# Two silu activations of a Mamba and mixture-of-experts kernel put into one block on ScalarE

## The chip, the cores and the metric

The kernel runs on one core of a Trainium2 chip. The metric is the device time of one execution in microseconds (us), lower being better. The program uses five engines of the core that run side by side and meet only at semaphores: TensorE (PE in the profile, with its weight loads as PEld), VectorE (DVE), ScalarE (ACT), GpSimd (POOL) and SyncE (SP), which here only starts transfers.

## The reference

The input is 32 sequences of 512 tokens with 256 features. A Mamba layer comes first and a mixture of 64 experts with a shared expert second, each after a layer norm and each added to its input. Cut to what the change is about:

```python
xz = xn @ in_proj_w.T
xp, z = xz[..., :D_INNER], xz[..., D_INNER:]
xc = silu(causal_conv(xp) + conv_b)
y = selective_scan(xc, softplus(dt), -exp(A_log), Bm, Cm, D)   # h = exp(dt*A)*h + dt*u*B ; y = <h, C>
m = gelu((y * silu(z)) @ out_proj_w.T)                          # silu of z
...
gu = x @ shared_gate_up_w
shared = silu(gu[:, :Is]) * gu[:, Is:] @ shared_down_w          # silu of the shared expert's gate
```

The scan has 512 channels (4 blocks of 128 partitions) and 16 states for each channel, so each sequence needs 64 scans of 128 x 512, done two at a time.

## The kernel before

The main part is a software pipeline over the 32 sequences. One turn handles the scan of sequence b, the preparation of sequence b+1 (`prep_at`: norm, projections of x and z, convolution, step sizes) and what comes after the scan of sequence b-1 (`post_at`: output projection, gelu, gated unit, second norm, router, shared expert). A turn has 32 half-steps (NS = 32, numbered s = 0 to 31), one for each pair of channel blocks and each of the 16 states. Each engine has a function `turn` of its own that walks through the 32 half-steps; the constants at the end of the file (`Z_AT`, `SILU_Z`, `SU_AT` and so on) say by hand in which half-step an engine issues which extra piece of work. An engine executes strictly in that order, and there is no planner. Turns 0, 1, 30 and 31 are written out, turns 2 to 29 are a hardware loop with two turns in its body, so there is a jump after every second turn. Turn 0 has no `post_at`, turn 31 no `prep_at`, so 30 turns have both.

In half-step s

- ScalarE first computes the decays of half-step s+2 (`decays`, L515, two activations into one of two PSUM buffers `state[n % 2]`). It must wait until VectorE has finished half-step s in that buffer (for the half-steps in `ON_POOL` the scan itself, otherwise the read-out).
- VectorE runs the scan (L1400), and in half-steps not in `ON_POOL` also the read-out with C (L1410). Among 25 to 31, the half-steps 25, 27, 28 and 29 are in `ON_POOL`.
- GpSimd makes the scan's inputs three half-steps ahead (L392) and does the read-outs of the half-steps in `ON_POOL` one half-step behind (L401).
- TensorE adds up the read-outs two half-steps behind (`add_up`, L907), then does the extra matmuls of `post_at`, then those of `prep_at`.

Around the change the hand-written order is this. The shared expert's gate is projected in half-steps 19, 20, 21 and 23 (`SG_AT`, L1015) and copied from PSUM by ScalarE one half-step later (`read_gate`, L673). `hid_silu` (L677) follows in half-step 24. The up-projections come in 25 to 28 (`SU_AT`, also L1015), and VectorE multiplies each one into `hid` one half-step later (`mul_up`, L1357), the first after waiting for `hid_ready`. The down-projection (`shared_down`, L1023) comes in 29 and 30 and is read by VectorE in 30 and 31 (`add_shared`, L1363). z is projected in 14, 21, 22 and 25 (`Z_AT`, L938), copied one half-step later (`read_z`, L579), and `silu_z` (L597) follows in 27. VectorE uses silu of z only in the next turn (`gate_y`, L1313). `choose` (L1341 to L1351, the router's top 8) stands on VectorE in half-step 25, `scales_x` (L520 to L527) on ScalarE in 26, `weights` (L660, L663) on ScalarE in 29.

Silu, and the exponential of the decays, need different activation tables. A switch is an instruction of its own, ACT_TABLE_LOAD: the load of the silu table stands at the line of the silu (L677, L597), the load back at L497, in `use_exp_ln`.

Of the kernel before, what the change touches and what calls it, by code (L numbers as in the profile page):

```python
# [40 lines left out]
def mamba_moe(nc, x, vectors, in_wT, conv_w, x_wT, dt_wT, a_log, out_wT, glu_wT, router_w, sgu_w, sdown_w, expert_w, out, counts, table, bc):  # L41
    ctx = ExitStack()
    with ctx:
# [451 lines left out]
        def _(act):  # L495
            def use_exp_ln():
                act.preload_act_table_set("natural_log_exp_and_others")  # L497
# [39 lines left out]
            def norm_x(p):  # L537
                act.wait_ge(scales0_ready, 5 * p + 5)
                wait(act, prep_full, (p - 1) * PREP_USES - FIRST + PREP_T[1] + 1)
                wait(act, post_read, (p - 1) * POST_USES - POST_USES)  # L540
                for i in range(NT):
                    m = act.activation(xn[:, i, :], xin[:, i, :], ACT.Identity, bias=shift[:, 1, i:i + 1],
                                       scale=rstd[:, 1, i:i + 1])
                m.then_inc(ln0, 1)

            def sum_x(p, h):
                wait(act, post_read, (p - 2) * POST_USES + POST_MT[1] + 1)
                for i in range(NT):
                    m = act.activation(xs[h][:, i, :], xin[:, i, :], ACT.Identity, bias=shift[:, 0, i:i + 1],
                                       scale=keep[:, i:i + 1])  # L550
                m.then_inc(xs_ready, 1)
# [9 lines left out]
            def read_xnT(p, f):  # L561
                act.wait_ge(prep_full, p * PREP_USES - FIRST + PREP_T[f] + 1)
                act.activation(xnT[:, f, :], prbank, ACT.Identity, bias=b_sb[:, f:f + 1],
                               scale=g_sb[:, f:f + 1]).then_inc(prep_read, 1)

            def begin_conv(p, h, j):
                act.wait_ge(prep_full, p * PREP_USES - FIRST + PREP_X[j] + 1)
                if j % JH == 0:
                    hf = j // JH
                    wait(act, summed, (p - 1 - hf) * NS + hf * N + 1)  # L570
                    wait(act, dt_ready, 4 * (p - 1 - hf) + 2 * hf + 1)
                act.activation(conv_part(h, j), prbank, ACT.Identity, bias=cb_sb[:, j:j + 1],
                               scale=cw_sb[:, j, PAD:TAPS]).then_inc(conv_begun, 1)

            def read_z(p, h, j):
                act.wait_ge(prep_full, p * PREP_USES - FIRST + PREP_Z[j] + 1)
                if j == 0:
                    wait(act, post_full, (p - 2) * POST_USES + POST_Y[J - 1] + 1)
                act.copy(sz[h][:, j, :], prbank).then_inc(prep_read, 1)  # L579

            def silu_x(p, h):
                act.wait_ge(prep_read, p * PREP_USES - FIRST + PREP_X[J - 1] + 1)
                both = xc3[:, h:h + 2, :, :]
                act.activation(both, both, ACT.Silu).then_inc(xc_ready, 1)
# [8 lines left out]
            def silu_z(p, h):  # L593
                if isinstance(p, int) and p == 0:
                    act.wait_ge(first_sz, J)
                wait(act, prep_read, p * PREP_USES - FIRST + max(PREP_Z) + 1)
                act.activation(sz[h][:, :, :], sz[h][:, :, :], ACT.Silu).then_inc(z_ready, 1)  # L597

            def read_xd(p):
                act.wait_ge(prep_full, p * PREP_USES - FIRST + PREP_S + 1)  # L600
                wait(act, bc_stored, 16 * p)
                act.copy(xd[0:64, :], prbank[0:64, :]).then_inc(prep_read, 1)

            def read_dt(p, j):
                act.wait_ge(prep_full, p * PREP_USES - FIRST + PREP_D[j] + 1)
                if j % JH == 0:
                    wait(act, input_ready, (p - 1) * NS + (j // JH + 1) * N)
                act.activation(dtu[:, j, :], prbank, ACT.Abs, bias=db_sb[:, j:j + 1])
                act.activation(dt[:, j, :], prbank, ACT.Relu, bias=db_sb[:, j:j + 1]).then_inc(prep_read, 1)  # L609
# [8 lines left out]
            def soft_log(p, hf):  # L618
                part = dtu[:, JH * hf:JH * hf + JH, :]
                act.wait_ge(soft, 4 * p + 2 * hf + 1)  # L620
                act.activation(part, part, ACT.Ln, bias=1.0).then_inc(soft, 1)
# [68 lines left out]
            def prep_at(p, h, s):  # L690
                if s == NORM0:
                    norm_x(p)
                if s == SUM_X:
                    sum_x(p, h)
                for f in range(FM):
                    if s == T_AT[f] + AFTER_T:
                        read_xnT(p, f)
                for j in range(J):
                    if s == X_AT[j] + AFTER_X:
                        begin_conv(p, h, j)  # L700
                    if s == Z_AT[j] + AFTER_Z:
                        read_z(p, h, j)
                if s == SILU_X:
                    silu_x(p, h)
                    use_exp_ln()
                if s == SILU_Z:
                    silu_z(p, h)
                    use_exp_ln()
                if s == S_AT + AFTER_S:
                    read_xd(p)  # L710
                for j in (0, 1):
                    if s == D_AT[j] + AFTER_D:
                        read_dt(p, j)
                if s == SOFT_AT[0][0]:
                    soft_exp(p, 0)
                if s == SOFT_AT[0][1]:
                    soft_log(p, 0)
                if s == SKIP_AT[0]:
                    scale_skip(p, h, 0)

            def post_at(q, h, s):
                for j in range(J):
                    if s == Y_AT[j] + AFTER_Y:
                        read_y(q, j)
                for f in range(FM):
                    if s == M_AT[f] + AFTER_M:
                        read_m(q, f)
                if s == M_AT[1] + AFTER_M:
                    gelu(q)
                    use_exp_ln()  # L730
                for f in range(FM):
                    if s == G_AT[f] + AFTER_G:
                        read_g(q, f)
                if s == G_AT[1] + AFTER_G:
                    glu_gate(q)
                    use_exp_ln()
                if s == SCALES2:
                    scales_x1(q)
                if s == NORM2:
                    norm_x1(q)  # L740
                for f in range(FM):
                    if s == XT_AT[f] + AFTER_XT:
                        read_x2T(q, f)
                for k in range(KS):
                    if s == SG_AT[k] + AFTER_SG:
                        read_gate(q, k)
                if s == SILU_HID:
                    hid_silu(q)
                    use_exp_ln()
                if s == ROUTER_EXP:  # L750
                    router_exp(q)
                if s == WEIGHTS:
                    weights(q)
                if s == C_AT + AFTER_C:
                    read_counts(q)

            def turn(b, h, prep, post):
                for s in range(NS):
                    to = ahead(b, h, s, 2, prep)
                    if to:  # L760
                        decays(*to)
                    second_steps(b, h, s)
                    if isinstance(b, int) and b == 0 and s == FIRST_SILU_Z:
                        silu_z(0, 0)
                        use_exp_ln()
                    if post:
                        post_at(b - 1, 1 - h, s)
                    if prep:
                        prep_at(b + 1, 1 - h, s)
                    if s == SCALES0 and not (isinstance(b, int) and b + 2 >= B):  # L770
                        scales_x(b + 2)

# [116 lines left out]
        def _(pe):  # L889
# [137 lines left out]
            def prep_at(p, h, s):  # L1027
# [3 lines left out]
                for j in range(J):  # L1031
                    if s == X_AT[j]:
                        project_in(p, PREP_X[j], j)
                    if s == Z_AT[j]:
                        project_z(p, j)
# [569 lines left out]
NORM2 = 16  # L1605
T_AT = (1, 3)
X_AT = (4, 5, 10, 12)
Z_AT = (14, 21, 22, 25)
SKIP_AT = (31, 14)
SILU_X = 14  # L1610
SILU_Z = 27
SILU_HID = 24
S_AT = 16
D_AT = (17, 18, 0, 1)
SOFT_AT = ((19, 21), (1, 3))
# [21 lines left out]
D_LATE = tuple(at + (NS if i >= JH else 0) for i, at in enumerate(D_AT))  # L1637
PREP_T, PREP_X, PREP_Z, (PREP_S,), PREP_D, PREP_USES = order(T_AT, X_AT, Z_AT, (S_AT,), D_LATE)
FIRST = PREP_USES - JH
# [39 lines left out]
```

## Time and profile before

| what | value |
|---|---|
| runs | 4388.48, 4369.52 and 4387.80 us; median 4387.8 us |
| profiled execution | 4384.62 us |
| its span, first to last instruction | 4381.6 us |
| mean granted TensorE clock | 0.893 of full speed |
| busy: GpSimd / VectorE / TensorE / ScalarE | 90% / 86% / 82% / 73% of the span |
| table loads at L497 / L597 / L677 | 159 / 32 / 31 |

Everything below is read from the profiled execution. Its time lies 3.0 us above its span, and 3.2 us below the median of the runs. In the timelines a line gives the start and the duration in us, then engine, line of the kernel, operation, output and input tiles, shapes and a count; a bracket at the end gives the idle time of the engine just before the instruction and the instruction that ended it. Several equal instructions in a row are merged.

### The profile page before, as it was taken

How to read it: one execution, taken by the hardware profiler on the slowest of the kernel's cores; microseconds unless marked ns; L12 is line 12 of the kernel's file. 1: busy time of each engine (PE TensorE's matmuls, PEld its weight loads, DVE VectorE, ACT ScalarE, POOL GpSimd, SP SyncE). 2: the span in 40 equal slices, each digit the busy share in tenths (PEclk: the TensorE clock that was granted, in tenths of full speed). 3: DMA queues.
4: the chain of work that ended last, by engine and by line, in shares of the span. 5: the costliest groups of instructions: out<-in, count | busy, mean ns of one | idle time of the engine just before them, and what ended most of it. 6: DMA issues, size and time to landing. Idle time of an engine off the chain costs nothing.

```text
span 4381.6 us, 54679 instructions
## 1 busy us (share of the span) xinstructions
PE 3579.6 (82%) x16225; PEld 2342.4 (53%) x16225; DVE 3752.6 (86%) x3728; ACT 3217.0 (73%) x5179; POOL 3951.1 (90%) x1931
## 2 busy tenths in 40 slices
PE   5788888888888888888888888888888888887765
PEld 3455555555555555555555555555555555554554
DVE  6899899898989989898998989898898989999432
ACT  6678777777777777777787777777777777776343
POOL 6999999999999999999999999999999999999266
PEclk8899989899989989998998989899898989998887
DMA  3232212133221222232222223222222322321576
GB/s 128 92 104 99 94 64 100 60 103 104 102 101 63 95 83 77 104 104 99 89 68 94 74 96 104 101 103 79 79 89 71 103 104 99 104 62 43 132 181 134
DMA packets 133417, 414.49 MB, mean 95 GB/s; under 512 B 21577, under 2 KB 80073, under 8 KB 100185
## 3 DMA queue, kind: packets, MB, share of 16 engines
q1 hardware_dynamic: 111720, 358.50, 22.4%
q0 software_dynamic: 21360, 51.92, 6.5%
q8 instruction: 161, 2.64, 0.2%
q14 instruction: 176, 1.43, 0.1%
HBM read 326.88 MB, written 50.46 MB: 86 GB/s over the span
## 4 chain that ended last, share of the span: by engine, by line
POOL 54%; issue 28%; PE 7%; DVE 5%; ACT 3%; DMA 3%; POOLq 1%; DVEq 0%; SPq 0%; ACTq 0%
POOL hs L392 33%; POOL hs L401 15%; POOL dtu L416 3%; DVE ps L1400 2%; DMA out<-hs,dt 2%; DVE hs L1400 1%; PE ps L907 1%; PE ps L1023 1%; POOL dt L411 1%; POOL out L474 1%; ACT ps L515 1%; PE ps L896 1%; PE ps L951 1%; DMA hs<-table,dt 1%; ACT L497 0%
## 5 line engine op out<-in xcount | busy, mean ns | idle before, releaser
L392 POOL TENSOR_TENSOR hs<-dtu,b_all 128x1024 f32<-128x1024 f32 x1024 | 2425.3, 2404 | 47.2 <-PE ps L907 44.7
L515 ACT ACTIVATE ps<-dt,neg_a 128x512 f32<-128x512 f32 x2048 | 1326.0, 683 | 437.9 <-DVE hs L1400 227.8
L1400 DVE TENSOR_TENSOR_SCAN hs<-ps,hs 128x1024 f32<-128x1024 f32 x512 | 1167.5, 2281 | 195.5 <-ACT ps L515 138.1
L907 PEld LDWEIGHTS ps<-ident,hs 128*128 128x128 f32 x8192 | 1038.7, 152 | 513.3 <-issue 401.3
L401 POOL TENSOR_TENSOR hs<-hs,c_all 128x1024 f32<-128x1024 f32 x512 | 1216.2, 2376 | 78.9 <-DVE hs L1400 78.9
L907 PE MATMUL ps<-ident,hs 128*128 128x128 f32 x8192 | 1168.1, 293 | 102.4 <-issue 58.0
L1400 DVE TENSOR_TENSOR_SCAN ps<-ps,hs 128x1024 f32<-128x1024 f32 x512 | 1170.0, 2285 | 74.0 <-ACT ps L515 69.9
L1410 DVE TENSOR_TENSOR hs<-ps,c_all 128x1024 f32<-128x1024 f32 x512 | 626.2, 1223 | 34.0 <-DVE ps L1400 6.6
L1015 PE MATMUL ps<-mT,w_sgu 128*128 128x512 f32 x992 | 482.9, 609 | 90.7 <-ACT hid L673 48.2
L931 PE MATMUL ps<-xnT,w_in 128*128 128x512 f32 x496 | 251.3, 631 | 81.6 <-DVE xc L1304 80.8
L1304 DVE SCALAR_TENSOR_TENSOR xc<-ps,cw_sb,xc 128x509 f32<-128x509 f32 (+2 forms) x384 | 285.3, 743 | 24.1 <-ACT xc L793 11.3
L1015 PEld LDWEIGHTS ps<-mT,w_sgu 128*128 128x128 f32 x992 | 168.7, 190 | 235.4 <-issue 119.1
L977 PE MATMUL ps<-mT,w_glu 128*128 128x512 f32 x496 | 242.5, 611 | 51.9 <-ACT mT L635 42.3
L938 PE MATMUL ps<-w_in,xnT 128*128 128x512 f32 x496 | 278.8, 691 | 3.7 <-ACT sz L579 3.7
L1023 PE MATMUL ps<-w_sd,hid 128*128 128x256 f32 x992 | 228.9, 384 | 16.3 <-DVE mT L1363 16.2
L968 PE MATMUL ps<-hid,w_out 128*128 128x512 f32 x496 | 223.3, 593 | 0.2 <-ACT hid L625 0.2
L1023 PEld LDWEIGHTS ps<-w_sd,hid 128*128 128x128 f32 x992 | 183.4, 190 | 48.4 <-DVE mT L1363 23.7
L497 ACT ACT_TABLE_LOAD x159 | 204.0, 1283 | 3.6 <-PEq L1649 0.8
L985 PE MATMUL ps<-ident,hid 128*128 128x128 f32 x248 | 59.2, 385 | 179.5 <-DVE xn L1325 178.1
L931 PEld LDWEIGHTS ps<-xnT,w_in 128*128 128x128 f32 x496 | 89.7, 191 | 203.7 <-DVE xc L1304 120.8
L951 PE MATMUL ps<-xd,w_dt 32*128 32x512 f32 x252 | 169.4, 757 | 23.7 <-ACT dt L609 21.8
L962 PE MATMUL ps<-ident,sz 128*128 128x128 f32 x496 | 96.4, 328 | 85.6 <-DVE sz L1313 63.9
(196 smaller groups left out, 4448.8 us busy)
## 6 DMA issues: line engine op xcount, KB each, us to landing
b_all<-bc SPq DMA_DIRECT2D x128, 1024.0 KB, 6.1
c_all<-bc SPq DMA_DIRECT2D x128, 1024.0 KB, 7.7
dt<-dtu POOLq DMA_DIRECT2D x63, 512.0 KB, 4.7
c_all<-expert_w SPq DMA_DIRECT2D x64, 384.0 KB, 3.9
table<-rows SPq DMA_DIRECT2D x32, 640.0 KB, 3.8
xin<-x SPq DMA_DIRECT2D x32, 512.0 KB, 3.6
out<-mT SPq DMA_DIRECT2D x32, 512.0 KB, 3.9
bc<-xd SPq DMA_DIRECT2D x32, 64.0 KB, 1.6
```

Source lines behind the costliest of these rows:

```text
L392: pool.tensor_tensor(ring(h, hf, n), dtu[:, JH * hf:JH * hf + JH, :], b_all[:, n, :].unsqueeze(1).broadcast_to([P, JH, L]), ALU.mult)\
L401: pool.tensor_tensor(ring(h, hf, n), ring(h, hf, n), c_all[:, n, :].unsqueeze(1).broadcast_to([P, JH, L]), ALU.mult)\
L515: i = act.activation(state_of(n)[:, k, :], dt[:, j, :], ACT.Exp, scale=neg_a[:, j, n:n + 1])
L907: m = pe.matmul(ybank[:, i, k * P:(k + 1) * P], ring(h, hf, n)[:, k, i * P:(i + 1) * P], ident[:, :], start=False, stop=(n == N - 1), is_t ...
L931: m = pe.matmul(prbank, w_in[:, f, col * P:(col + 1) * P], xnT[:, f, :], start=(f == 0), stop=(f == FM - 1))
L938: m = pe.matmul(prbank, xnT[:, f, i * P:(i + 1) * P], w_in[:, f, DI:2 * DI], start=(f == 0), stop=(f == FM - 1))
L977: m = pe.matmul(pobank, w_glu[:, k, col:col + P], mT[:, k, :], start=(k == 0), stop=(k == FM - 1))
L1015: m = pe.matmul(pobank, w_sgu[:, f, block * P:(block + 1) * P], x2T[:, f, :], start=(f == 0), stop=(f == FM - 1))
L1023: m = pe.matmul(po_tok[:, i, :], hid[:, k, (2 * c + i) * P:(2 * c + i + 1) * P], w_sd[:, k, :], start=(k == 0), stop=(k == KS - 1))
L1304: dve.scalar_tensor_tensor(conv_part(h, j)[:, back:L], bank[:, 0:L - back], cw_sb[:, j, k:k + 1], conv_part(h, j)[:, back:L], ALU.mult, AL ...
L1400: dve.tensor_tensor_scan(inputs if s in ON_POOL else whole, whole, inputs, 0.0, ALU.mult, ALU.add).then_inc(state_ready, 1)
L1410: dve.tensor_tensor(ring(h, hf, n), state_of(n), c_all[:, n, :].unsqueeze(1).broadcast_to([P, JH, L]), ALU.mult)\
```

## The change

`hid_silu` and `silu_z` move from half-steps 24 and 27 into half-step 25, one behind the other, with one load of the exponential table behind both in place of one behind each. So that z is complete by then, its last projection moves from half-step 25 to 24, and the copy that follows it from 26 to 25. In half-step 25 ScalarE then issues in this order: decays of half-step 27, `hid_silu` (from `post_at`), the copy of the last part of z and `silu_z` (from `prep_at`), `use_exp_ln`.

```diff
                 if s == SILU_X:
                     silu_x(p, h)
                     use_exp_ln()
-                if s == SILU_Z:
+                if s == SILU_BOTH:
                     silu_z(p, h)
-                    use_exp_ln()
...
-                if s == SILU_HID:
+                if s == SILU_BOTH:
                     hid_silu(q)
-                    use_exp_ln()
...
                     if prep:
                         prep_at(b + 1, 1 - h, s)
+                    if s == SILU_BOTH:
+                        use_exp_ln()
...
-Z_AT = (14, 21, 22, 25)
+Z_AT = (14, 21, 22, 24)
...
-SILU_Z = 27
-SILU_HID = 24
+SILU_BOTH = 25
```

## Rows read from the trace of the kernel before

**Rows 1.** The page: busy times, and the chain that ended last, by line.

```profile
PE 3579.6 (82%) x16225; PEld 2342.4 (53%) x16225; DVE 3752.6 (86%) x3728; ACT 3217.0 (73%) x5179; POOL 3951.1 (90%) x1931
...
POOL hs L392 33%; POOL hs L401 15%; POOL dtu L416 3%; DVE ps L1400 2%; DMA out<-hs,dt 2%; DVE hs L1400 1%; PE ps L907 1%; PE ps L1023 1%; POOL dt L411 1%; POOL out L474 1%; ACT ps L515 1%; PE ps L896 1%; PE ps L951 1%; DMA hs<-table,dt 1%; ACT L497 0%
```

**Rows 2.** Table of waits, whole run: waiter, releaser, total us, times, longest.

```profile
DVE ps L1400 <- ACT ps L515: 69.9, 88, 3.0
```

**Rows 3.** Timeline of ScalarE in half-steps 24 to 29 of one turn.

```profile
2028.08 1.30 ACT L515 ACTIVATE ps<-dt,neg_a 128x512 f32<-128x512 f32 x2 [0.36 <-DVE hs L1410]
...
2029.92 1.28 ACT L677 ACT_TABLE_LOAD   x1
2031.21 1.91 ACT L677 ACTIVATE hid<-hid 128x2048 f32<-128x2048 f32 x1
...
2036.96 0.57 ACT L579 COPY sz<-ps 128x512 f32<-128x512 f32 x1
...
2038.51 1.30 ACT L515 ACTIVATE ps<-dt,neg_a 128x512 f32<-128x512 f32 x2 [0.31 <-DVE hs L1400]
...
2041.12 1.92 ACT L597 ACTIVATE sz<-sz 128x2048 f32<-128x2048 f32 x1
2043.06 1.28 ACT L497 ACT_TABLE_LOAD   x1
2044.36 2.53 ACT L515 ACTIVATE ps<-dt,neg_a 128x512 f32<-128x512 f32 x4
```

**Rows 4.** Timeline of VectorE in half-steps 25 to 31 of the same turn.

```profile
2027.96 2.28 DVE L1400 TENSOR_TENSOR_SCAN hs<-ps,hs 128x1024 f32<-128x1024 f32 x1
...
2035.60 0.68 DVE L1357 TENSOR_TENSOR hid<-ps,hid 128x512 f32<-128x512 f32 x1
2036.19 2.28 DVE L1400 TENSOR_TENSOR_SCAN hs<-ps,hs 128x1024 f32<-128x1024 f32 x1
...
2038.97 2.28 DVE L1400 TENSOR_TENSOR_SCAN hs<-ps,hs 128x1024 f32<-128x1024 f32 x1
...
2043.95 0.67 DVE L1357 TENSOR_TENSOR hid<-ps,hid 128x512 f32<-128x512 f32 x1
2045.69 2.30 DVE L1400 TENSOR_TENSOR_SCAN ps<-ps,hs 128x1024 f32<-128x1024 f32 x1 [1.07 <-ACT ps L515]
...
2049.16 0.87 DVE L1363 SCALAR_TENSOR_TENSOR mT<-ps,small,xn 128x256 f32<-128x256 f32 x2
...
2053.84 0.88 DVE L1363 SCALAR_TENSOR_TENSOR mT<-ps,small,xn 128x256 f32<-128x256 f32 x2 [0.35 <-PE ps L1023]
```

**Rows 5.** Timeline of TensorE in the same turn.

```profile
2028.98 1.91 PE L907 MATMUL ps<-ident,hs 128*128 128x128 f32 x16
2030.73 1.88 PE L1015 MATMUL ps<-mT,w_sgu 128*128 128x512 f32 x4
2032.45 1.88 PE L938 MATMUL ps<-w_in,xnT 128*128 128x512 f32 x4
...
2050.09 3.72 PE L1023 MATMUL ps<-w_sd,hid 128*128 128x256 f32 x16 [0.39 <-DVE mT L1363]
```

**Rows 6.** Timeline of VectorE in turn 31, which has no `prep_at`.

```profile
4049.19 0.67 DVE L1357 TENSOR_TENSOR hid<-ps,hid 128x512 f32<-128x512 f32 x1
...
4053.83 0.88 DVE L1363 SCALAR_TENSOR_TENSOR mT<-ps,small,xn 128x256 f32<-128x256 f32 x2 [0.51 <-PE ps L1023]
```

**Rows 7.** Timeline of GpSimd behind a jump, and behind a turn's end without one.

```profile
2061.24 2.34 POOL L401 TENSOR_TENSOR hs<-hs,c_all 128x1024 f32<-128x1024 f32 x1 [0.98 <-DVE hs L1400]
...
2073.97 2.36 POOL L392 TENSOR_TENSOR hs<-dtu,b_all 128x1024 f32<-128x1024 f32 x1 [3.43 <-PE ps L907]
...
2216.42 2.35 POOL L401 TENSOR_TENSOR hs<-hs,c_all 128x1024 f32<-128x1024 f32 x1 [0.77 <-DVE hs L1400]
```

**Rows 8.** Line L497 (ns min/median/max, first to last start); ScalarE, 4150 to 4380 us, by line.

```profile
L497 ACT ACT_TABLE_LOAD  x159: 1283/1283/1283, 0.8 to 4076.9; - x159
...
L837 ACT ACTIVATE hs<-ps 128x128 f32<-128x128 f32 x56 | 15.5, 277 | 50.6 <-PE ps L1162 48.0
```

## The prediction

> **What bounds the kernel now.** I read the page first. GpSimd is the busiest engine, and its two lines L392 and L401 carry half of the chain that ended last; ScalarE, from which the change takes work, is busy 73% of the time [rows 1]. By this alone a gain on ScalarE would be worth nothing. But the chain only says where GpSimd was busy; it does not say what GpSimd waits for in its gaps. So next came GpSimd's timeline. In each round of the loop (two turns) there are gaps, and the three that stand behind a turn's end lead back to VectorE. Behind a jump GpSimd waits 0.98 us for a scan and 3.43 us for a sum on TensorE, which itself waits there for VectorE's `gate_y`; behind the other turn's end it waits 0.77 us for a scan [rows 7]. In front of that last wait VectorE runs from the turn's end on almost without a gap. So the moment at which VectorE gets through the end of a turn passes on to everything later, in either kind of turn, and I take a shift of that moment at one to one.
>
> What holds VectorE up at the end of a turn is seen in its timeline: 1.07 us before the scan of half-step 30, for ScalarE's decays, and 0.35 us before the second `add_shared`, for the down-projection on TensorE [rows 4]. The first repeats in every turn that I looked at, and belongs to the 69.9 us that scans of this form wait for decays in the whole run [rows 2]. ScalarE's timeline shows why: behind the decays of half-step 29, which end at 2039.81, stand a load, silu of z and a load, and the decays of 30 begin only at 2044.36 [rows 3].
>
> **What the change removes.** In the 30 turns with both silus one load of the silu table and one load back go: 60 loads of 1.283 us [rows 8], 77 us of ScalarE's busy time. Each of them is worth something only as far as VectorE waits for what stands behind it.
>
> **What it moves, on ScalarE.** Times are those of the turn of rows 3 to 5. The decays of 27 now stand ahead of the block. They wait for the scan of 25, which ends at 2027.96 + 2.28 = 2030.24 [rows 4]; decays follow a scan by 0.04 us (2038.51 after 2036.19 + 2.28) and take 1.30 [rows 3, 4], so they end at 2031.58. Then come load 1.28, silu 1.91, copy 0.57, silu 1.92, load 1.28 [rows 3]: 6.96, with four seams of about 0.01 to 0.02 and one overlap of about 0.06 some 6.98. The decays of 28 begin at 2038.56, and a scan starts 1.33 after the start of its decays (2044.36 to 2045.69) [rows 3, 4]: the scan of 28 starts at 2039.89. Before it started at 2038.97 without a wait [rows 4]. So the longer block brings a **new wait of 0.92 us** in half-step 28. Queued behind the block are the decays of 28, `scales_x` (under 1.0 us, as it lies between the copy's end at 2037.53 and 2038.51 before [rows 3]) and the decays of 29, which end near 2042.2, in time for the scan of 29 at 2041.75 + 0.92 = 2042.67; and the decays of 30, which need only the scan of 28 (ends 2042.17) and are ready near 2043.5. So the **old wait of 1.07 us** in half-step 30 goes. VectorE's last `mul_up` moves from 2043.95 to 2044.87, a scan follows a `mul_up` by 0.59 (2035.60 to 2036.19) [rows 4], and the scan of 30 starts at 2045.46, 0.23 earlier than before.
>
> **What is late next.** The down-projection on TensorE needs that last `mul_up`, which is now 0.92 later. Before, VectorE's own order hid it, since the wait came behind the `mul_up`. Now the `mul_up` ends at 2045.54, the down-projection takes 3.72 [rows 5], and with 0.08 for the two hand-overs the first `add_shared` can start at 2049.34. VectorE is there at 2049.16 - 0.23 = 2048.93 and waits. So it starts 0.18 later than the 2049.16 of before. The other end of this term is turn 31, where `prep_at` is missing and no wait for decays stands between: there the first `add_shared` starts 4.64 after the last `mul_up`, and waits 0.51 for TensorE [rows 6]; 2044.87 + 4.64 = 2049.51 is 0.35 later than before. The difference is how TensorE's sum of 27, which stands between the last up-projection and the down-projection, lies. I take 0.25, between both. The second down-projection starts when the first `add_shared` is done, and takes as long as before, so the turn's end moves by the same 0.25.
>
> **The edits that I cost at nothing.** Silu of the gate ends at 2031.58 + 1.28 + 1.91, near 2034.8, in place of 2033.12. The first `mul_up` waits for it, and stands at 2035.60 behind VectorE's read-out [rows 4]: 0.8 us are left, and beyond them each microsecond would cost 30. The projection of z in half-step 24 goes between the two sums that are one merged row at 2028.98, from about 2029.9 to 2031.8, and pushes the second sum and the first up-projection back by 1.7 to 1.9; that one ends near 2034.4 in place of 2032.6 [rows 5], also ahead of 2035.60. The copy of z in the block at 2034.8 finds its matmuls done 3 us before. The sums that go later are needed by GpSimd's inputs eight half-steps on, so they are covered as well. GpSimd does its read-outs of 28 and 29 behind other work of its own, several microseconds after the scans; that covers the 0.92. On SP the order stays the same: the store of the rows waits for `weights`, which comes a little earlier, and the transfers behind it with it. Silu of z is used in the next turn only.
>
> **The sum.** 30 turns x 0.25 = 7.5 us, between 5.4 (0.18) and 10.5 (0.35). The two turns with one silu change by a microsecond or so. The profiled execution took 4384.6 us, so the sum is **4392 us**. The median of the runs is 3.2 above the profiled execution, the lowest run 15 below it; I leave 4392 as it is and put this scatter into the range.
>
> The Trainium skill (ScalarE: Activation LUTs, section "What ACT_TABLE_LOAD costs") gives 1283 ns for the load, and 1380 ns for a drain beside it. Here the trace agrees on the load but shows no drain: the silu starts 1.29 us after the start of its load [rows 3]. With a drain of 1.38 us behind both loads of the block the Trainium skill would make the block 2.76 us longer and the sum 30 x 2.76 = 83 us higher; the sum goes by the trace.
>
> **The rivals.** (a) *The freed time arrives.* The down-projection does not bind, for instance because TensorE has done its sum of 27 and its weight loads run ahead; the turn's end then moves with the scan of 30, by -0.23: 30 x 0.23 = -7 us, 4378 us. For it speaks that the first `add_shared` waits for nothing before, against it turn 31. (b) *Grouping pays in full.* The new wait does not appear, since decays of 28 come 0.92 earlier than I worked out, and both old waits go: 30 x (1.07 + 0.35) = -43 us, 4342 us. The block would have to end within what two scans, a read-out, `choose` and two multiplications cover; against it stands that every piece of the block has a row. The Trainium skill's rule to group activations by table set (ScalarE: Activation LUTs, section "Table sets: the hidden batching unit") would make this the outcome; the trace agrees that each switch saved is 1.28 us of ScalarE, not that VectorE waits for all of it. (c) *The long block is paid in full, the kernel gets slower.* ScalarE computes no decays for 7 us, and there are two buffers only. If it does not catch up in half-steps 28 to 30, the 0.92 stays on VectorE: 30 x 0.92 = 28 us, 4412 us. It decides from where the decays of 29 end later than 2042.67, half a microsecond later than I have them. (d) *The change doesn't do what it says.* A load could stand between the two silus, because of the copy. 30 x (0.25 + 1.28) = +46 us, 4430 us. Against it: in the last stage silu (L837) alternates with copies on ScalarE, 56 times in the window of rows 8, and the last load of the exponential table is at 4076.9 [rows 8].
>
> **How the numbers follow.** A measurement of this kernel can tell about 0.5% from no change, here 22 us. Forecast 0.74, (a) 0.12, (b) 0.04, (c) 0.07, (d) 0.03. Forecast and (a) lie within 0.5%, together 0.86; (b) is faster, 0.04; (c) and (d) are slower, 0.10. The range takes in (a), less a little for the scatter of the runs, and (c): 4373 to 4413.
>
> **What would show it.** In the profile after: 129 loads at L497 in place of 159, and 33 loads at L677 and L597 in place of 63, ScalarE's busy time near 3140 us. A wait for decays of 0.9 us at the scan of 28, none at the scan of 30. A wait of a few tenths for L1023 at both `add_shared` of a turn, in all 30 turns, where before there was one at the second. A round of the loop longer by 0.3 to 0.7 us. I am wrong if the first `mul_up` waits for silu, if the scan of 30 still waits for decays, or if VectorE's shift at a turn's end does not show in the length of the round.

## The result and the profile after

The kernel after the change took 4345.05 us (median), the kernel before 4371.97 us in the same runs: ratio 0.9928, 95% interval 0.9913 to 0.9943. It is 0.7% faster, below the predicted range of 4373 to 4413 us, and the sign is wrong. The profiled execution of after took 4338.69 us (span 4336.4, mean granted clock 0.902), that of before 4384.62. These two lie 46 us apart, but the medians 27 us, and the ratio stands for 31 us: the runs of the unchanged kernel spread from 4345 to 4388 us and its profiled execution is near their upper end, while those of after lie between 4337 and 4350. One run of after at a lower granted clock (4411 us, 0.84) counts neither in the ratio nor in this range. The spread of before turns out to be the key.

The page of after: busy times and the table loads of the exponential [rows 1, 8].

```profile
PE 3561.0 (82%) x16225; PEld 2310.4 (53%) x16225; DVE 3755.3 (87%) x3728; ACT 3135.9 (72%) x5119; POOL 3948.8 (91%) x1931
...
L497 ACT ACT_TABLE_LOAD x129 | 165.5, 1283 | 3.2 <-PEq L1648 0.8
```

ScalarE is busy 81 us less, with 30 loads less at L497 and 30 less at the silus. That is what the edit does, and the other engines issue as many instructions as before.

ScalarE's timeline of after at the block, in turn 15, the turn of [rows 3] (start, duration, engine, line, operation).

```profile
2007.92 0.59 ACT L673 COPY hid<-ps 128x512 f32<-128x512 f32 x1 [0.47 <-PE ps L1015]
2008.40 1.31 ACT L515 ACTIVATE ps<-dt,neg_a 128x512 f32<-128x512 f32 x2
2009.72 1.28 ACT L677 ACT_TABLE_LOAD   x1
2011.02 1.91 ACT L677 ACTIVATE hid<-hid 128x2048 f32<-128x2048 f32 x1
2012.84 0.57 ACT L579 COPY sz<-ps 128x512 f32<-128x512 f32 x1
2013.44 1.91 ACT L597 ACTIVATE sz<-sz 128x2048 f32<-128x2048 f32 x1
2015.37 1.28 ACT L497 ACT_TABLE_LOAD   x1
2016.66 1.30 ACT L515 ACTIVATE ps<-dt,neg_a 128x512 f32<-128x512 f32 x2
```

The block takes 2016.66 - 2009.72 = 6.94 us, as worked out (6.98), and no load stands between the two silus. VectorE's timeline of after from there to the jump, beside [rows 4]:

```profile
2018.00 2.29 DVE L1400 TENSOR_TENSOR_SCAN hs<-ps,hs 128x1024 f32<-128x1024 f32 x1 [1.07 <-ACT ps L515]
...
2023.56 2.29 DVE L1400 TENSOR_TENSOR_SCAN ps<-ps,hs 128x1024 f32<-128x1024 f32 x1
...
2027.46 0.88 DVE L1363 SCALAR_TENSOR_TENSOR mT<-ps,small,xn 128x256 f32<-128x256 f32 x2 [0.35 <-PE ps L1023]
...
2032.15 0.88 DVE L1363 SCALAR_TENSOR_TENSOR mT<-ps,small,xn 128x256 f32<-128x256 f32 x2 [0.35 <-PE ps L1023]
2036.54 2.29 DVE L1400 TENSOR_TENSOR_SCAN hs<-ps,hs 128x1024 f32<-128x1024 f32 x1 [3.51 <-issue]
```

The new wait at the scan of half-step 28 is there, the wait at the scan of 30 is gone, and both `add_shared` wait for the down-projection. So the end of the turn behaves as predicted, and is not where the time went. That is seen when the starts of the 32 scans are counted from the first scan of their turn and averaged over turns 4 to 27. "Even" turns stand behind a jump, "odd" ones in front of it; the numbers are waits of VectorE in us, before to after. The last column is taken from the starts of the scans, so it also holds what the instructions between two scans wait.

| place | even turns | odd turns | sum per round |
|---|---|---|---|
| jump, before the first scan of the even turn | 4.23 to 3.46 | | -0.77 |
| scan of half-step 5 | 1.11 to 0.31 | 0.20 to 0.00 | -1.09 |
| scan of half-step 20 | 0.83 to 0.44 | 0.32 to 0.17 | -0.54 |
| scan of half-step 21 | 1.99 to 1.99 | 2.00 to 0.33 | -1.66 |
| half-steps 28 to 31 together (shift of the turn's end) | +0.18 | +0.44 | +0.62 |

The sum is -3.44 us per round; a round of these turns is 252.6 us long before and 249.1 after, on average. Added up over the 14 rounds of the loop, that is the 46 us between the profiles. Everything gained lies in places that the edit doesn't touch: the jump, and half-steps 5 to 21. GpSimd's wait for a sum behind the jump, 3.43 us in [rows 7], is now 2.92 in its timeline:

```profile
2051.12 2.37 POOL L392 TENSOR_TENSOR hs<-dtu,b_all 128x1024 f32<-128x1024 f32 x1 [2.92 <-PE ps L907]
```

**The jump.** SP's queue and VectorE's scan behind the jump of before, then SP's store of after, whose scan stands above (turn 15 to 16 in both).

```profile
2048.34 0.40 SPq L301 DMA_DIRECT2D table<-rows  x1
2048.86 0.43 SPq L293 DMA_DIRECT2D b_all<-bc  x1
2049.49 0.87 SPq L297 DMA_DIRECT2D c_all<-bc  x1
...
2058.88 2.29 DVE L1400 TENSOR_TENSOR_SCAN hs<-ps,hs 128x1024 f32<-128x1024 f32 x1 [4.15 <-POOL hs L392]
```

```profile
2025.87 0.40 SPq L301 DMA_DIRECT2D table<-rows  x1
```

The turn ends at 2053.84 + 0.88 = 2054.72 [rows 4] and at 2033.03. So the store of the rows and the two transfers of 1 MB behind it start 6.38 us ahead of the turn's end before, 7.16 after: the store waits for `weights`, ahead of which ScalarE now has no silu and no load. The two 1 MB transfers follow within 1.2 us in both. DMA queues of before from the turn's end on, in the stretches 2054.7 to 2056.6 and 2056.6 to 2058.9 (packets, MB, share of the 16 engines):

```profile
q1 hardware_dynamic: 103, 0.81, 100.9%
...
q1 hardware_dynamic: 304, 0.11, 18.2%
q8 instruction: 1, 0.02, 3.6%
q14 instruction: 2, 0.02, 1.7%
```

While the transfers fill the engines, no packet of an instruction queue (q8, q14) moves. Behind them these come, and VectorE scans at 2058.88, 2.3 us after 2056.6. In after the engines are full until 2034.2 (a share of 100.0% from 2033.0 on, no instruction packet), the instruction packets come behind, and the scan follows at 2036.54, again 2.3 us later. At all 13 jumps of all twelve profiles (before, after and the ten runs below) the same is seen: no instruction packet in the last 9 us of the turn, the first one 0.2 to 2.9 us behind its end, and the scan 2.0 to 2.9 us behind that packet. So the jump waits for code, and the code waits for the two transfers; the experiments test that. The label of the wait is no hint: it names GpSimd in one line and "issue" in the other.

**The clock.** Half-step 21 in odd turns, before, turn 15: TensorE, ScalarE and VectorE, then the granted clock (the number in front of the DMA share, 1.00 is 2.4 GHz) between 2006 and 2009.

```profile
2005.89 1.92 PE L896 MATMUL ps<-ident,xc 128*128 128x128 f32 x8
2007.60 1.92 PE L907 MATMUL ps<-ident,hs 128*128 128x128 f32 x8
...
2011.19 1.12 PE L951 MATMUL ps<-xd,w_dt 32*128 32x512 f32 x2
...
2012.35 0.69 ACT L608 ACTIVATE dtu<-ps,vecs 128x512 f32<-128x512 f32 x1 [1.90 <-PE ps L951]
...
2014.84 2.29 DVE L1400 TENSOR_TENSOR_SCAN hs<-ps,hs 128x1024 f32<-128x1024 f32 x1 [2.00 <-ACT ps L515]
...
2006.00:2009.00 3.00, 3.00 (x15) 3.00 (x16) 2.68 (x2) 3.00 (x6) 3.00 (x2) 0.50 0.02 5
```

The same of after, turn 15:

```profile
1985.42 1.09 PE L896 MATMUL ps<-ident,xc 128*128 128x128 f32 x8
1986.35 1.04 PE L907 MATMUL ps<-ident,hs 128*128 128x128 f32 x8
...
1989.06 1.12 PE L951 MATMUL ps<-xd,w_dt 32*128 32x512 f32 x2
...
1992.70 2.29 DVE L1400 TENSOR_TENSOR_SCAN hs<-ps,hs 128x1024 f32<-128x1024 f32 x1 [0.33 <-ACT ps L515]
...
1986.00:1989.00 3.00, 3.00 (x29) 2.98 (x27) 2.82 (x2) 3.00 (x7) 3.00 (x3) 1.00 0.00 0
```

The two small groups ahead of the second `project_dt` (L951) take 1.92 us each at 1.2 GHz and 1.09 and 1.04 at 2.4 GHz. The step sizes are that much later, ScalarE waits for them with the decays of 21 queued behind, and VectorE pays 1.67 us. Half-step 5 of even turns is of the same kind: behind the jump the clock is at 0.50, in before until about 2074.3 (15.4 us after the first scan), in after until about 2050.2 (13.7 us). At the 52 jumps of before, after and the first two runs below, the wait at 5 is at most 0.58 us where the clock is back within 14.0 us of the first scan, and 0.73 to 1.51 us where it takes 14.8 us or more. ScalarE's copy for the gate of z there, before and after:

```profile
2074.57 0.59 ACT L625 COPY hid<-ps 128x512 f32<-128x512 f32 x1 [1.90 <-PE ps L962]
```

```profile
2051.45 0.59 ACT L625 COPY hid<-ps 128x512 f32<-128x512 f32 x1 [1.03 <-PE ps L962]
```

### The profile page after: what moved, and what is told of

Same layout as the page of the kernel before. It is cut to its first block, busy times and chain, and to the rows that moved or that the text cites. A ratio compares the mean times of both kernels' runs of the same rounds, so it can differ in the third digit from the quotient of the medians.

```text
span 4336.4 us, 54619 instructions
## 1 busy us (share of the span) xinstructions
PE 3561.0 (82%) x16225; PEld 2310.4 (53%) x16225; DVE 3755.3 (87%) x3728; ACT 3135.9 (72%) x5119; POOL 3948.8 (91%) x1931
## 4 chain that ended last, share of the span: by engine, by line
POOL 48%; issue 23%; PE 14%; DVE 7%; ACT 4%; DMA 3%; POOLq 1%; SPq 0%; DVEq 0%; ACTq 0%
POOL hs L392 30%; POOL hs L401 13%; POOL dtu L416 3%; PE ps L907 3%; DVE hs L1400 3%; PE ps L1015 2%; DMA out<-hs,dt 2%; DVE ps L1400 2%; PE ps L1023 2%; PE ps L946 1%; ACT ps L515 1%; PE ps L938 1%; POOL dt L411 1%; DVE xc L1304 1%; POOL out L474 1%
## 5 line engine op out<-in xcount | busy, mean ns | idle before, releaser
L907 PEld LDWEIGHTS ps<-ident,hs 128*128 128x128 f32 x8192 | 1025.1, 150 | 503.7 <-issue 426.7
L907 PE MATMUL ps<-ident,hs 128*128 128x128 f32 x8192 | 1150.6, 290 | 82.1 <-issue 46.1
L1015 PE MATMUL ps<-mT,w_sgu 128*128 128x512 f32 x992 | 507.4, 636 | 96.0 <-DVE hid L1357 57.6
L1023 PEld LDWEIGHTS ps<-w_sd,hid 128*128 128x128 f32 x992 | 183.4, 190 | 37.7 <-DVE mT L1363 10.3
L951 PE MATMUL ps<-xd,w_dt 32*128 32x512 f32 x252 | 171.2, 763 | 24.7 <-ACT dt L609 22.2
L474 POOL DMA_INDIRECT out<-hs,dt x64 | 103.8, 1621 | 65.9 <-DMA out<-hs,dt 36.9
```

The source lines that it names most:

```text
L907: m = pe.matmul(ybank[:, i, k * P:(k + 1) * P], ring(h, hf, n)[:, k, i * P:(i + 1) * P], ident[:, :], start=False, stop=(n == N - 1), is_t ...
L1015: m = pe.matmul(pobank, w_sgu[:, f, block * P:(block + 1) * P], x2T[:, f, :], start=(f == 0), stop=(f == FM - 1))
L1023: m = pe.matmul(po_tok[:, i, :], hid[:, k, (2 * c + i) * P:(2 * c + i + 1) * P], w_sd[:, k, :], start=(k == 0), stop=(k == KS - 1))
```

## The experiments

The first question was whether the gain comes from the silus at all, and whether it needs the change.

**The kernel before once more, and z alone.** The first has no edit. The second is

```diff
-Z_AT = (14, 21, 22, 25)
+Z_AT = (14, 21, 22, 24)
```

> The kernel before, unchanged, profiled a second time. All theories: VectorE waits 1.07 us for decays at the scan of half-step 30 in each turn. Theory T (what follows the end of a turn sets the time: the jump, and where TensorE's stretches at 1.2 GHz lie in the round): the runs of before scatter from 4345 to 4388 us because rounds of the loop come in a longer (252.6 us) and a shorter kind, so a second profile may show some rounds near 249 us. Rival R (the time goes with ScalarE's work alone): all rounds alike, 252.6 us.

> Only z's last projection and its copy move up by a half-step; both silus stay in half-steps 24 and 27 with four loads. Theory T: the transfers behind `weights` and the wait of 1.07 us in half-step 30 stay where they were, so the jump stays at 4.2 us of VectorE's time and the kernel stays within 0.2% of before. Rival Z (the changed place of TensorE's z projection moves its stretches at 1.2 GHz, and that is the gain): 0.6 to 0.8% faster, wait in half-step 21 of the odd turns down from 2.0 to about 0.3 us.

Measured: 1.0003 (0.998 to 1.0025) and 0.9997 (0.9974 to 1.0019). The projection of z is worth nothing that these runs can tell. But the profile of the unchanged kernel holds both kinds of round in one execution: turns 2 to 11 have rounds of 248.4 to 250.1 us, turns 12 to 27 rounds of 252.1 to 253.3. In turn 7 of it (granted clock 0.67 from 989 to 992 us), then in turn 9 (1.00 from 1239 to 1242):

```profile
989.63 1.65 PE L896 MATMUL ps<-ident,xc 128*128 128x128 f32 x8
991.08 1.91 PE L907 MATMUL ps<-ident,hs 128*128 128x128 f32 x8
...
998.56 2.29 DVE L1400 TENSOR_TENSOR_SCAN hs<-ps,hs 128x1024 f32<-128x1024 f32 x1 [1.99 <-ACT ps L515]
...
1239.24 1.10 PE L896 MATMUL ps<-ident,xc 128*128 128x128 f32 x8
1240.17 1.04 PE L907 MATMUL ps<-ident,hs 128*128 128x128 f32 x8
...
1246.52 2.29 DVE L1400 TENSOR_TENSOR_SCAN hs<-ps,hs 128x1024 f32<-128x1024 f32 x1 [0.34 <-ACT ps L515]
```

Counted over turns 3 to 28 of before, after and these two, and of two more runs below, 156 turns in all: the scan of 21 waits 1.98 to 2.00 us in every turn in which a stretch at 1.2 GHz begins between 73 and 78 us after the first scan (107 turns), and 0.14 to 0.34 in every turn in which none does (49). The profiled execution of z alone had short rounds throughout (248.7 to 249.9, a span of 4345.3, among the lowest of its runs, whose median is 4376) although its jump takes 4.06 and scan 30 still waits 1.08. So the pattern of the clock, not the silus, makes a round long or short, and before falls into either. Its spread goes with that: of 61 runs of the unchanged kernel whose granted clock is known, the eight up to 4360.4 us have 0.900 to 0.903, the others, from 4362.8 us on, 0.899 or less, those above 4380 us 0.891 to 0.895. In the profiles of z alone and of after every even turn has the long wait at 21 and every odd turn the short one, so what the rest of the change does can be read there apart from that pattern: per round, after is 0.62 us shorter at the jump and 0.43 longer at half-steps 27 to 31, and its mean round is 0.07 us shorter.

**`weights` one half-step earlier, in the kernel before.**

```diff
-WEIGHTS = 29
+WEIGHTS = 28
```

> The kernel before, with `weights` in half-step 28 in place of 29, so that the store of the rows and the two transfers of 1 MB behind it on SP start about 1.1 us earlier against the end of the turn; the silus, their loads and z stay. Theory T: the jump of VectorE gets shorter by 0.7 to 1.1 us (4.2 to about 3.3) and most of the gain is there: 0.3 to 0.8% faster. Rival R (the silu block itself is the gain): no change, within 0.2%.

Measured 0.9935 (0.9911 to 0.9959), 4346 us, runs from 4344.7 to 4348.7. VectorE at scan 30 and behind the jump, and SP's store (the turn ends at 2033.64):

```profile
2024.62 2.30 DVE L1400 TENSOR_TENSOR_SCAN ps<-ps,hs 128x1024 f32<-128x1024 f32 x1 [1.07 <-ACT ps L515]
...
2036.33 2.29 DVE L1400 TENSOR_TENSOR_SCAN hs<-ps,hs 128x1024 f32<-128x1024 f32 x1 [2.69 <-issue]
...
2026.05 0.40 SPq L301 DMA_DIRECT2D table<-rows  x1
```

The whole gain comes without touching a silu; both loads and the wait of 1.07 are still there. The jump takes 2.75 us on average, less than the 3.3 that were expected. An earlier `weights`, and with it an earlier store, is enough; the next run moves the store alone.

**The change, with the store held back.** SP waits for VectorE's read-out of half-step 30 ahead of the store:

```diff
                 if post:
+                    wait_apart(sp, readout_ready, vector_reads(b, 31))
                     store_rows(b - 1)
```

> The kernel after, silu block and all, but SP holds the store of the rows, and with it the two transfers of 1 MB behind it, until VectorE's read-out of half-step 30 is done. They then start about 5.9 us ahead of the turn's end, where after has 7.2 and before 6.4. Theory T (the transfers' place against the jump is what the change gained by): the jump goes from 3.5 back to 4.2 to 4.8 us of VectorE's time, and the kernel is about as slow as before, within 0.4% of it, in spite of the block. Rival R (the silu block and the saved loads are the gain): as after, 0.7% faster than before, since VectorE never waits for the store.

Measured 1.0024 (0.9999 to 1.0049), 4385 us: the gain is gone with the silu block in place. SP and VectorE (turn's end at 2054.15):

```profile
2048.48 0.40 SPq L301 DMA_DIRECT2D table<-rows  x1
...
2058.94 2.29 DVE L1401 TENSOR_TENSOR_SCAN hs<-ps,hs 128x1024 f32<-128x1024 f32 x1 [4.79 <-issue]
```

The store starts 5.67 us ahead of the turn's end and the jump takes 4.8. Of 13 odd turns 6 have the long wait at 21 again, and rounds of 251 and 254 us alternate. What is left, 0.24% or 10 us above before, has the size that I had predicted for the block, but it doesn't confirm it: the interval takes in no change, and this kernel's jump is also 0.58 us longer than that of before.

**The loads kept.** The load of the exponential table stands between the two silus again, so the block has the two loads of before:

```diff
                 if s == SILU_BOTH:
                     hid_silu(q)
+                    use_exp_ln()
```

> The kernel after, with the two loads put back between the two silus, so that the order is that of after and the loads are those of before. Theory T: the block is 2.57 us longer, the scan of 28 waits 3.4 us in place of 0.9, and the end of each turn comes 2.5 us later than in after: +75 us, 1.7% slower than after, about 1% slower than before; the jump stays at 3.5 us. Rival (ScalarE's loads do not matter at all since it has idle time): as after, 0.7% faster than before.

Measured 1.0287 (1.0259 to 1.0314), 4501 us: 156 us above after, where 75 were expected. VectorE in half-steps 28 to 30 (the lines lie one further down in this kernel):

```profile
2094.08 2.29 DVE L1401 TENSOR_TENSOR_SCAN hs<-ps,hs 128x1024 f32<-128x1024 f32 x1 [3.52 <-ACT ps L515]
...
2100.82 0.69 DVE L1358 TENSOR_TENSOR hid<-ps,hid 128x512 f32<-128x512 f32 x1 [1.68 <-PE ps L1016]
...
2106.00 0.88 DVE L1364 SCALAR_TENSOR_TENSOR mT<-ps,small,xn 128x256 f32<-128x256 f32 x2 [1.02 <-PE ps L1024]
```

The two loads make scan 28 2.45 us later (3.52 for 1.07), as expected. On top of that the last `mul_up` and the first `add_shared` wait for TensorE, so the turn's end goes back by 3.6 to 3.9 us in each turn, 7.4 per round; and the odd turns have the long wait at 21 again, the waits of half-steps 4 to 21 together 3.6 per round more. The jump takes 0.66 less on average, where 3.5 as in after was expected. It comes in two kinds within this one profile: 3.48 where the store lies 7.16 ahead of the turn's end, as in after (6 jumps), and 2.30 where it lies 9.62 ahead (7 jumps). 7.4 + 3.6 - 0.7 = 10.3 per round, some 155 us over 15. So within one block leaving the two loads out is worth double their own 77 us, a third of it at the waits of half-steps 4 to 21; against two blocks, as in before, it is worth nothing that these runs show.

**Still earlier.** After, with `WEIGHTS = 28` as above:

> The kernel after with `weights` in half-step 28, so that the transfers start earlier still. Theory T: the jump goes from 3.5 to about 2.7 us, as in the kernel before with the same edit; with 13 jumps 10 us, 0.2 to 0.4% faster than after, 1.0% faster than before. Rival (the instruction fetch needs its 3.5 us anyway once it is out of the transfers' way): as after.

Measured 0.9938 (0.992 to 0.9957), 4346 us, the same as after. The jump takes 2.3, but the 1.2 us won come back at once, for the decays of half-steps 3 to 5 (here 4 and 5):

```profile
2050.45 2.29 DVE L1400 TENSOR_TENSOR_SCAN hs<-ps,hs 128x1024 f32<-128x1024 f32 x1 [0.37 <-ACT ps L515]
2053.54 2.30 DVE L1400 TENSOR_TENSOR_SCAN ps<-ps,hs 128x1024 f32<-128x1024 f32 x1 [0.79 <-ACT ps L515]
```

The rounds stay at 249.2. The theory that a shorter jump arrives one to one falls here, and the expected 0.2 to 0.4% did not come.

Seven kernels with their store, the first packet of an instruction queue and their jump (us, means over the 13 jumps of a profile):

| kernel | store ahead of the turn's end | first instruction packet behind it | wait at the jump | runs, lowest to highest |
|---|---|---|---|---|
| after, store held | 5.67 | 2.60 | 4.80 | 4377 to 4399 |
| before (all runs beside after) | 6.38 | 1.85 | 4.22 | 4345 to 4388 |
| z alone | 6.43 | 1.81 | 4.06 | 4346 to 4388 |
| after | 7.16 | 1.13 | 3.47 | 4337 to 4350 |
| after, loads kept | 7.16 or 9.62 | 1.22 or 0.29 | 3.48 or 2.30 | 4499 to 4503 |
| before, `WEIGHTS = 28` | 7.61 | 0.70 | 2.75 | 4345 to 4349 |
| after, `WEIGHTS = 28` | 9.94 | 0.27 | 2.29 | 4337 to 4350 |

The wait falls about one to one with the store, down to some 2.2. What an early store takes away are the long runs (but not where the loads are kept); it makes no run shorter than the short ones of before, but for some 8 us.

**The wait of half-step 21 by itself.** If TensorE's order there costs up to 2 us per turn, moving something should win it. First the second step sizes one half-step later, in before and in after with `WEIGHTS = 28`:

```diff
-D_AT = (17, 18, 0, 1)
+D_AT = (17, 19, 0, 1)
```

> The kernel before with the second step-size projection in half-step 19 in place of 18, so that the decays of half-step 21 stand ahead of its copy on ScalarE's queue. Theory T (the wait of 2.0 us at the scan of half-step 21 is ScalarE behind TensorE's project_dt, which is late when TensorE runs at 1.2 GHz there): the wait is 0 to 0.3 us in all turns whatever the clock, 1.2 to 2% faster than before. Rival (the wait belongs to something else, or comes back in the next half-steps): within 0.3% of before.

> The kernel after with `weights` in half-step 28 and the second step-size projection in half-step 19. If both mechanisms hold and add up: 2% faster than before (4285 us). If they are the same gain seen twice (only the place of the stretches at 1.2 GHz in the round counts): no faster than the better one of the two edits alone.

Measured 1.0269 (1.0235 to 1.0303) and 1.0226 (1.0192 to 1.026). Theory T expected a gain in the first and missed, as did its rival; the second shows no sum of two gains. The wait at 21 is 0, and larger ones stand behind it (at 22 and 24, on average 2.4 and 1.2 us in the first); VectorE of the first at half-step 22:

```profile
2197.88 2.29 DVE L1400 TENSOR_TENSOR_SCAN hs<-ps,hs 128x1024 f32<-128x1024 f32 x1 [3.67 <-ACT ps L515]
```

Then the router's logits (L1001), which stand ahead of L951, one half-step later in after; and the same with VectorE's and ScalarE's reading of them left in its place, by

```diff
-R_AT = 18
+R_AT = 19
...
-AFTER_R = 2
+AFTER_R = 1
```

> The kernel after with the router's logits on TensorE in half-step 19 in place of 18, so that they no longer stand between the sum and the second step-size projection (L951) on TensorE's queue; VectorE reads them one half-step later. Theory T (the wait at the scan of half-step 21 is ScalarE behind L951, and this is late by the 0.8 us that each of the two groups ahead of it takes longer at 1.2 GHz): L951 starts 2 us earlier in either pattern, the wait of 2.0 us in the even turns goes to about 0 and the 0.33 in the odd ones too, up to 2 us for each round, 0.4 to 0.6% faster than after. Rival (the time comes back behind, as with the projection in half-step 19, because the logits are late for what follows): as after or slower.

> As the run before, but VectorE reads the logits in half-step 20 as in after, so it waits for them there. Theory T: the scan of 21 waits less for ScalarE, but VectorE waits about 1.4 us for the logits instead; in the even turns about 0.5 us gained, in the odd ones about 1 us lost: within 0.3% of after. Rival (early logits matter more than L951): faster than the run before.

Measured 1.0174 (1.0141 to 1.0206) for the logits alone, where theory T expected a gain: what reads them goes back too (waits of 1.02 at 21, 0.70 at 24). Measured 0.9931 (0.99 to 0.9962), 4340 us, with the reading left in its place: the same as after, as expected. TensorE and VectorE of the second, in an even turn:

```profile
2110.48 1.91 PE L896 MATMUL ps<-ident,xc 128*128 128x128 f32 x8
2112.18 1.91 PE L907 MATMUL ps<-ident,hs 128*128 128x128 f32 x8
2114.03 1.12 PE L951 MATMUL ps<-xd,w_dt 32*128 32x512 f32 x2
...
2117.94 0.43 DVE L1334 COPY lg<-ps 128x260 f32<-128x260 f32 x1 [1.31 <-PE ps L1001]
2118.74 2.28 DVE L1400 TENSOR_TENSOR_SCAN hs<-ps,hs 128x1024 f32<-128x1024 f32 x1
```

The two groups still take 1.91 at the low clock (granted 0.51 from 2110.5 to 2113.8), but L951 no longer stands behind L1001, and the scan of 21 waits for decays in no turn, though in 25 of the 26 turns 3 to 28 a stretch at 1.2 GHz begins in the same place (73 to 78 us). Now VectorE waits for the logits instead. Even turns gain 0.9 us, odd ones lose about as much. No version beats after by more than the runs can tell.

## Why the prediction was wrong, point by point

The block of silus did to the end of a turn what was worked out. Two steps around it failed: the edit on SP that was costed at nothing, and the shift that was taken to pass on one to one.

- **The block and the new wait: right.** 6.94 for 6.98. The wait at 28 is 0.81 in even turns and 1.07 in odd ones, for 0.92. The odd ones are longer because ScalarE's copy ahead of the decays of 27 waits 0.47 for TensorE (first line of the block above), which I had left out.
- **The old wait goes, the down-projection binds: right.** The wait at 30 is 0 in all turns, both `add_shared` wait 0.35. The turn's end moves by +0.18 and +0.44, for +0.25 predicted between 0.18 and 0.35. Over 30 turns that is 9.3 us, for 7.5.
- **No drain: right.** The Trainium skill (ScalarE: Activation LUTs, section "What ACT_TABLE_LOAD costs") has 1380 ns beside the load; the silu here starts 1.30 us after the start of its load, the decays 1.29 after theirs, and each load starts 0.01 to 0.02 us after the end of the instruction ahead of it.
- **The edits costed at nothing: here it failed.** "On SP the order stays the same: the store of the rows waits for `weights`, which comes a little earlier, and the transfers behind it with it" was the right observation, and I gave it no price. 0.78 us on SP are 0.77 us at the jump, some 10 us over 13 jumps, which alone takes back the 9.3 us of the turns' ends. I had these transfers and the jump in the profile, and did not lay one against the other: the transfers are what the jump waits for.
- **"Passes on to everything later, one to one": here it failed as well, by more.** I took the waits at half-steps 5, 20 and 21 as fixed. They became 3.3 us per round shorter, they depend on where TensorE is at 1.2 GHz, and the unchanged kernel changes them from round to round. The prediction's own sign of being wrong came: the later end of the turn does not show in the round, which is 3.4 us shorter in place of 0.3 to 0.7 longer.
- **The spread of the runs: misread.** I put 15 us below the profile down to scatter. It was a kernel with two lengths of round, whose profiled execution had the long one. So the sum started from 4384.6 us, where the median of before in the same runs as after is 4371.97.
- **Rival (b) gave 4342 us**, close to the result, but by a mechanism that did not happen: the wait at 28 came, the waits at `add_shared` doubled. That it came close is luck. The rule of the Trainium skill named there (group activations by table set) is not what made this kernel faster either: with the store held the grouping gives nothing (1.0024).

**What is shown and what stays open.** Shown: holding the store takes the gain away, an earlier `weights` with its store gives it without the silus, the jump follows the store, and the wait at 21 goes with the clock in all 156 turns. Not shown: how an earlier store brings the clock's pattern into the short kind. A short jump is not sufficient (with the loads kept the jump is 2.85 and the wait at 21 is long) and not needed (z alone, with a jump of 4.06). With `WEIGHTS = 28` in before the turns are mixed and the rounds still short on average. Why after has the short kind in every odd turn and the long one in every even turn was not settled. One regularity of the profiles was not used above: the mean rounds (turns 4 to 27) take only a few lengths. They are 249.1 to 249.3 us in after, z alone, both kernels with only `WEIGHTS = 28` added and the last run, 252.6 in before and with the store held, 256.0 with the logits alone, 259.4 and 259.5 with the step sizes moved in before and with the loads kept: steps of 3.4 us, though the edits differ by other amounts. Two profiles lie between (251.6 and 257.9), with rounds of both neighbouring lengths in them. Single rounds alternate about the mean in some of them. It looks as if a small gain shows here as nothing or as a whole step; no run tests what sets the step.

## What to carry to other kernels

Ahead of a loop's jump, see which transfers are in flight: here the code came by the same DMA engines, and an edit that moved two large transfers against the jump by 0.78 us moved the jump by as much, on a queue that the prediction had costed at nothing. When runs of one kernel spread by more than the effect sought, compare the rounds within one profile before anything else; the spread may be two patterns, and the change may do no more than choose between them. An edit on a critical engine should be followed through every queue that it releases, not only to the next wait on its own.

## What the runs showed of the hardware

- At a jump of the hardware loop no packet of the instruction queues moves while the two 1 MB transfers fill the 16 DMA engines; VectorE resumes 2.3 us after they end (before and after, turn 15), and with the transfers out of the way the jump costs 2.2 to 2.5 us (after with `WEIGHTS = 28`). In the run with the store held the instruction packets do move beside smaller packets of data (83% of the 16 engines between 2056.6 and 2059.0 us).
- TensorE does nothing from 2056.7 to 2058.7 at the jump of before and stands at 1.2 GHz for some 15 us behind it; each group of 8 small matmuls there takes 1.9 to 2.1 us in place of 1.0 to 1.1.
- A stretch at 1.2 GHz of a few us costs nothing or 1.67 us, by whether it falls on the two groups ahead of the step sizes.
